# Graph attention on one core: edge chunks of 512 become 1024, node ranges 32 become 42, and the last stage is spread over the engines in another way

## The reference

```python
Q_h = (x @ Wq + bq).reshape(N, H, D)          # N 12500, H 8, D 12
K_h = (x @ Wk + bk).reshape(N, H, D)
V_h = (x @ Wv + bv).reshape(N, H, D)
E = (edge_attr @ We + be).reshape(-1, H, D)
src = K_h[src_idx]
dest = Q_h[dst_idx]
score = src * dest / sqrt(D) * E
score = exp(clip(score.sum(-1, keepdims=True), -5.0, 5.0))
msg = V_h[src_idx] * score
wV = segment_sum(msg, dst_idx, num_segments=N)
Z = segment_sum(score, dst_idx, num_segments=N)
h_out = wV / (Z + 1e-06)
out = layernorm(x + h_out)
```

## Time and profile before

| what | us |
|---|---|
| median of 3 runs (lowest, highest) | 5353.9 (5344.9, 5357.64) |
| the profiled execution | 5341.94 |
| its span in the trace | 5340.3 |
| busy: PE, DVE, ACT, POOL | 3563.3, 2090.0, 1722.8, 3143.5 |
| first gather of the loop's steady part to the last one | 143.44 to 5217.30 |
| last stage | 5245.00 to 5340.30 |

### The profile page before, as it was taken

How to read it: one execution, slowest core, us unless ns; L and a number is a source line. 1 busy time by engine, 2 the same in 40 slices (tenths; PEclk the granted TensorE clock), 3 DMA queues, 4 the chain that set the end, 5 groups by cost and what they waited for, 6 DMA issues and landing times.

```text
span 5340.3 us, 72730 instructions
## 1 busy us (share of the span) xinstructions
PE 3563.3 (67%) x19972; PEld 3422.0 (64%) x19973; DVE 2090.0 (39%) x5996; ACT 1722.8 (32%) x3602; POOL 3143.5 (59%) x3249
## 2 busy tenths in 40 slices
PE   7666666666666666666666666666666666666664
PEld 6666666666666666666666666666666666666663
DVE  4333334333333333333333433333334333433346
ACT  4332333323332332333233332333333232323337
POOL 4556656665666656656665666566566665666560
PEclk7555555555555555555555555555555555555555
DMA  7444444444444444444444444444444444444442
GB/s 227 107 109 110 119 109 109 111 118 109 109 111 117 110 108 111 116 111 109 111 116 112 109 112 113 113 109 111 110 118 109 110 115 113 109 110 116 112 109 84
DMA packets 497768, 607.49 MB, mean 114 GB/s; under 512 B 256053, under 2 KB 420224, under 8 KB 497630
## 3 DMA queue, kind: packets, MB, share of 16 engines
q0 software_dynamic: 155200, 318.39, 22.5%
q1 hardware_dynamic: 233215, 281.36, 18.0%
q10 hardware_dynamic: 109330, 7.48, 1.5%
HBM read 584.51 MB, written 22.46 MB: 114 GB/s over the span
## 4 chain that ended last, share of the span: by engine, by line
PE 51%; issue 27%; another core or an unknown queue 13%; DVE 4%; ACT 2%; DVEq 1%; DMA 0%; ACTq 0%; POOL 0%; SPq 0%; POOLq 0%
PE bank L633 18%; PE bank L647 17%; PE bank L631 11%; PE bank L640 5%; DVE kqe L915 2%; DVE raw_score L926 1%; DVEq L303 1%; ACT spare L814 0%; DVE oh L910 0%; ACT spare L802 0%; ACT accP L792 0%; PE bank L597 0%; ACT eaT L760 0%; DVE kqe L907 0%
## 5 line engine op out<-in xcount | busy, mean ns | idle before, releaser
L530 POOL DMA_INDIRECT kv<-kv_table,src_idx x3224 | 3118.9, 967 | 2059.6 <-DVE msg L919 1020.4
L633 PE MATMUL bank<-w_e,eaT 97*128 97x96 f32 x6448 | 1886.1, 391 | 282.1 <-issue 282.1
L631 PE MATMUL bank<-ident,ea 128*96 128x128 f32 x3224 | 1354.9, 421 | 920.4 <-issue 610.5
L633 PEld LDWEIGHTS bank<-w_e,eaT 97*128 97x128 f32 x6448 | 1778.6, 333 | 290.4 <-issue 288.8
L907 DVE TENSOR_TENSOR kqe<-kv,bank 128x384 f32<-128x384 f32 x806 | 446.4, 554 | 3157.5 <-remote 2428.7
L631 PEld LDWEIGHTS bank<-ident,ea 128*96 128x96 f32 x3224 | 806.2, 250 | 928.7 <-issue 594.5
L647 PE MATMUL bank<-oh,msg 128*104 128x32 f32 x6448 | 1276.8, 355 | 172.3 <-issue 170.0
L647 PEld LDWEIGHTS bank<-oh,msg 128*104 128x104 f32 x6448 | 1225.4, 290 | 168.7 <-issue 166.0
L757 ACT ACTIVATE msg<-score 128x32 f32<-128x32 f32 x806 | 184.8, 229 | 3504.8 <-remote 2565.3
L640 PEld LDWEIGHTS bank<-q_win,ohT 96*128 96x128 bf16 x3224 | 398.3, 154 | 414.5 <-issue 408.2
L640 PE MATMUL bank<-q_win,ohT 96*128 96x96 bf16 x3224 | 448.5, 279 | 299.6 <-issue 295.5
(11 more groups left out here) (81 smaller groups left out, 525.8 us busy)
## 6 DMA issues: line engine op xcount, KB each, us to landing
ea<-in_edge_attr_dram SPq DMA_DIRECT2D x201, 768.0 KB
dst_b<-dst_by_chunk SPq DMA_DIRECT2D x201, 384.0 KB
kv<-kv_table,src_idx POOLq DMA_INDIRECT x3224
q_win<-q_table SPq DMA_DIRECT2D x806, 19.9 KB
kv_table<-kv_out SPq DMA_DIRECT2D x25, 336.0 KB
q_table<-q_out SPq DMA_DIRECT2D x25, 252.0 KB
spare<-in_x_dram SPq DMA_DIRECT2D x25, 168.0 KB
out_dram<-spare SPq DMA_DIRECT2D x25, 168.0 KB
```

What stands on the lines that cost most here:

```text
L530: pool.indirect_dma_start(kv[:, slot, g, :], None, kv_dram[:, :], bass.IndirectOffsetOnAxis(ap=src_idx[:, u, g:g + 1], axis=0)).then_inc(k ...
L631: last = nc.tensor.transpose(eaT_ps[u % 2][0:D, g * P:(g + 1) * P], ea[:, u, g, :], ident[:, :])
L633: nc.tensor.matmul(e_ps[v % 2][:, g * D:(g + 1) * D], eaT[:, v % 2, g * P:(g + 1) * P], w_e[:, :], start=True, stop=True)
```

## The change

Chunks have 1024 edges (`G` = 8, `C` = 403) and node ranges 42 nodes. Rings have 4 slots (`RING`), halves 2 (`HALF`), so they hold as many edges as before. The pipeline is arranged anew: a PE step `s` turns chunk s and raises `pe_turned`, sums chunk s - 2, picks the Q rows of chunk s, projects chunk s, and raises `pe_projected`. `eaT`, `eaT_ps`, `e_ps` and `q_ps` have one buffer each, of twice the size. ACT's step waits on `pe_turned`, DVE's and SP's on `pe_projected`. DVE's step computes scores and messages of the same chunk. In the last stage PE turns `accT` directly, POOL adds the residual, and mean and variance come from DVE's `bn_stats` and `bn_aggr`. In the diff, the parts are those of SP, POOL, PE, DVE in the loop, and DVE in the last stage, in this order.

```diff
-G = 4
+G = 8
+GB = 4
 CHUNK = P * G
-WIN = 32
+WIN = 42
-PROJ_LAG = 2
-SUM_LAG = 5
+SUM_LAG = 2
-RING = 8
+RING = 4
 HALF = RING // 2
+ROUND = 8
...
             def half_round(s, h, bases):
-                sp.wait_ge(pe_step, s - HALF + PROJ_LAG)
+                sp.wait_ge(pe_projected, s - HALF)
                 sp.sem_inc(loads_allowed, 1)
...
+            def add_residual(b, u):
+                pool.wait_ge(y_attended, b + 1)
+                wait_batch(pool, x_res_in, b, u)
+                nc.gpsimd.tensor_tensor(y[0:NP, u, :, :], y[0:NP, u, :, :], x_res[0:NP, u, :, :], ALU.add).then_inc(res_added, 1)
...
             def step(s, u, _):
-                c, v = s - PROJ_LAG, (u - PROJ_LAG) % RING
-                n, w = s - SUM_LAG, (u - SUM_LAG) % RING
+                n, w = s - SUM_LAG, (u - SUM_LAG) % 2
...
+                    for g in range(G):
+                        last = nc.tensor.transpose(eaT_ps[0:D, g * P:(g + 1) * P], ea[:, u, g, :], ident[:, :])
+                    last.then_inc(pe_turned, 1)
                 if summing:
                     pe.wait_ge(msg_ready, n + 1)
                     at_least(pe, acc_added, n - 1)
...
+                if whole:
+                    pe.wait_ge(ohT_built, s + 1)
+                    at_least(pe, kqe_done, s)
+                    landed(pe, q_win_in, s, u, 16)
...
+                        nc.tensor.matmul(edge_rows(q_ps, g), sel[:, g, :], q_win[0:SEL, u, :],
+                                         start=(g % GB == 0), stop=(g % GB == GB - 1), skip_group_check=True)
+                    pe.wait_ge(eaT_copied, s + 1)
+                    for g in range(G):
+                        last = nc.tensor.matmul(edge_rows(e_ps, g), eaT[:, g * P:(g + 1) * P], w_e[:, :],
+                                                start=True, stop=True)
-                last.then_inc(pe_step, 1)
+                last.then_inc(pe_projected, 1)
...
             def step(s, u, base):
-                dve.wait_ge(pe_step, a + PROJ_LAG + 1)
+                dve.wait_ge(pe_projected, s + 1)
...
+                    dve.wait_ge(heads_summed, s + 1)
+                    nc.vector.tensor_scalar(score[:, h, :], raw_score[:, :], -5.0, 5.0, ALU.max, ALU.min).then_inc(score_ready, 1)
+                    dve.wait_ge(exp_done, s + 1)
+                    nc.vector.tensor_tensor(msg[:, h, :, 0:D].rearrange("p g (h d) -> p g h d", d=HD),
...
                 if second:
-                    dve.wait_ge(squared, b)
-                    nc.vector.tensor_reduce(sq_sum[0:NP, v % 2, :], ysq[0:NP, v % 2, :, :], AX_X, ALU.add).then_inc(sq_summed, 1)
+                    dve.wait_ge(res_added, b)
+                    for j in range(BATCH):
+                        last = nc.vector.bn_stats(y_stats[0:NP, v % 2, j, :], y[0:NP, v, j, :])
+                    last.then_inc(stats_made, 1)
```

More of the change, by code:

```diff
@@ L31 @@
 NP16 = 112
+NQ16 = 96
 BATCH = 4
@@ L39, in at_least, with run_steps @@
         engine.wait_ge(sem, value)
-def run_steps(engine, step, chunks, lag, round_values=None, from_round=0, unroll=RING, ahead=0):
+def run_steps(engine, step, chunks, lag, round_values=None, from_round=0, unroll=ROUND, ahead=0):
     rounds = (chunks - 1 - ahead) // unroll
@@ L223, in gnn_kernel @@
         kv_in = [sem(f"kv_in{i}") for i in range(RING)]
-        pe_step = sem("pe_step")
+        pe_turned = sem("pe_turned")
+        pe_projected = sem("pe_projected")
         eaT_copied = sem("eaT_copied")
@@ L335, in within @@
         def within(node):
-            return nc.s_assert_within(node, 0, N - 1, skip_runtime_bounds_check_because=
-                                      "a chunk's windows end with the one that holds its greatest destination")
+            return nc.s_assert_within(node, 0, N_PAD - WIN, skip_runtime_bounds_check_because=
+                                      "a chunk's windows end with the one that holds its greatest destination or the next")
         def load_sources(engine, s, u):
@@ L626, in step @@
-                if projecting:
-                    pe.wait_ge(eaT_copied, c + 1)
-                    at_least(pe, kqe_done, c - 1)
-                for g in range(G):
-                    if turning:
-                        last = nc.tensor.transpose(eaT_ps[u % 2][0:D, g * P:(g + 1) * P], ea[:, u, g, :], ident[:, :])
-                    if projecting:
-                        nc.tensor.matmul(e_ps[v % 2][:, g * D:(g + 1) * D], eaT[:, v % 2, g * P:(g + 1) * P],
-                                         w_e[:, :], start=True, stop=True)
@@ L660, in add_queries @@
                     for g in range(G):
-                        last = nc.tensor.matmul(q_ps[0][:, g * D:(g + 1) * D], sel[:, g, :], q_win[0:SEL, 0, :],
-                                                start=first and g == 0, stop=(g == G - 1), skip_group_check=True)
+                        last = nc.tensor.matmul(edge_rows(q_ps, g), sel[:, g, :], q_win[0:SEL, 0, :],
+                                                start=first and g % GB == 0, stop=(g % GB == GB - 1), skip_group_check=True)
                     last.then_inc(f_q_added, 1)
@@ L754, in step @@
+            def step(s, u, _):
+                c, v = s - 1, (u - 1) % 2
+                coming = not isinstance(s, int) or s + 1 < C
+                if not isinstance(s, int) or s < C:
+                    act.wait_ge(pe_turned, s + 1)
+                    nc.scalar.copy(eaT[0:D, :], eaT_ps[0:D, :]).then_inc(eaT_copied, 1)
+                if coming:
+                    measure(s + 1, (u + 1) % RING)
                 if not isinstance(s, int) or 0 <= c < C:
                     act.wait_ge(score_ready, c + 1)
-                    nc.scalar.activation(msg[:, v % 2, :, D:DZ],
-                                         score[:, v % 2, :].rearrange("p (g h) -> p g h", g=G), ACT.Exp).then_inc(exp_done, 1)
@@ L930, in step @@
+                if not isinstance(s, int) or 0 <= n < C:
                     if base is None:
```

362 lines of the change are left out of this document (171 added, 191 removed).

## The result

The changed kernel takes 5725.56 us (median of 4, 5720.45 to 5741.11) against 5353.2: ratio 1.0701, 95% interval 1.0677 to 1.0725. The prediction was 5765. The profiled execution's span is 5721.7 us against 5340.3, so 381.4 us more.

The account below looks back on a forecast made before the run. The prediction took the loop as bound by PE's signals held until POOL's run of gathers ends, then DVE's chain before POOL restarts. 5341.9 + 439 + 5 - 8 - 24 = 5754, 5765 for the median; range 4600 to 5900.

Parts of the forecast that it names:

- The chain: DVE's work from PE's signal to the messages, uncovered while POOL's queue is empty: 4.7 us a period, against 1.69 before.
- The restart: POOL's time from DVE's messages to its next gather: 0.81 us a period.
- The first signal after a release: PE's signal due 0.9 us into the next run of gathers was to come on time.
- The release: Time from a run's last gather until PE's held signal reaches DVE: 2.29 us, as before.
- The sum of a period: Steady loop: 19.79 + 2.29 + 4.7 + 0.81 = 27.6 us against 25.56, put at +2.2, times 199.5 periods: +439 us.
- lower bound of 4600: Lower end of the forecast range, taking in mid-run cases down to a release at 16.5 us.
- The second signal: PE's next signal, 20.8 us into a run ending at 19.79, was to come with the release at 22.1 us.
- the first rival: PE's second signal comes in mid-run: total between 4270 and 5330 us, 4840 at the middle; chance 0.24.
- DVE holding POOL: Rival: DVE's message product in each run slows gathers, +65 to +100 us, up to 5865; chance 0.09.
- First chunks: Loop's start: the first step takes a whole 1024-edge chain, about +5 us.
- Last chunks: After the last gather: two PE steps at 8.5 us and the chain, about 20 us against 27.7: -8 us.
- The last stage: 25 batches after the loop, DVE at 2.7 us a batch: -24 us, with bounds of 0 and -45.

Follow-up runs that it names:

- e5: Changed kernel with POOL's gathers of chunk s also waiting for pe_projected of chunk s-3, and DVE's oh and accT add behind the clip: 5109.4 us, 0.9547 of the kernel before.
- c0: The changed kernel with no edit, as a base: 5714.1 us, 1.0681 of the kernel before.
- e1: Changed kernel with one more wait on POOL, gathers of chunk s also waiting for pe_projected of chunk s-3: 5114.8 us, 0.9383 of the kernel before.
- e10: Changed kernel with POOL filling 2048 columns after every 8 gathers, run where the kernel before takes 5351 us: 5291.4 us, 0.9892 of the kernel before.
- e2: Changed kernel with DVE's oh and add into accT moved behind the clip: 5619.1 us, 1.0285 of the kernel before.
- e3: Changed kernel with gathers of 96 floats a row instead of 192, so half the bytes: 5916.2 us, 1.0843 of the kernel before.
- e4: Changed kernel with PE's and DVE's loops unrolled over 4 chunks in place of 8: 5914.1 us, 1.0839 of the kernel before.
- e7: Changed kernel with ACT's exponential of chunk s-1 ahead of its wait for pe_turned of chunk s: 5906.0 us, 1.1026 of the kernel before.
- e8: Changed kernel with POOL filling 2048 columns of an unused tile after every 8 gathers: 5300.8 us, 1.2398 of a kernel before that took 4274.2 us.
- e9: Changed kernel with POOL filling 256 columns of an unused tile after each gather: 5302.8 us, 1.2403 of a kernel before that took 4274.2 us.
- e6: Kernel before with POOL also waiting, every second chunk of 512 edges, for the step that projects chunk s-5: 5174.4 us, 0.9665 of the kernel before.

## Why the prediction was right, and where it was off

**What bounds the loop** was read rightly: DVE's chain in POOL's idle time behind a signal held to the run's end. The gap at 2410.20 shows its three parts, the pauses' sum grew by 477.2 us, and with the chain beside gathers the kernel takes 605 us less (e5 against c0; e1 reached 5115 without DVE's other order). That PE's signals are held while gathers are issued, late in a run, and come out in a pause is shown by the phases (180 of 182, then 9 of 199) and by e10. The length of the chain itself was never changed by an experiment, as e2 missed; its share rests on the 4.73 us of the gaps. By what means the signals are held stays open.

**The chain**: 4.7 predicted, 4.73 measured. **The restart**: 0.81 and 0.81. **The first signal after a release**, due 0.9 us into the run by the prediction, was due at 1.1 and came on time.

**The release** was the term of the period that moved: 2.29 taken over from before, 1.56 at 2410.20, median 2.9 over the loop.

**The sum of a period** has a slip. 19.79 + 2.29 + 4.7 + 0.81 is 27.59, which is 2.03 more than 25.56 and not 2.2: the run falls from 20.77 to 19.79, by 0.98, where only the inner gap of 0.8 was counted. By its own terms the loop's growth is 405 us and not 439, so 34 of the 66 us by which the steady loop was missed are this slip. Nor is the period of before that was read the only kind: 135 of the steady loop's 218 runs have 16 gathers and 76 have 12. Its 25.56 agrees with the mean of 25.43 all the same. The lower bound of 4600 for a release at 16.5 us comes out at 4645 when it is worked out again.

**The second signal**: predicted to come with the run's end. It does in 155 of the 188 runs, which have 16 gathers; 27 runs have 24, as one signal came in mid-run, the first rival in part, and in 21 of the 187 gaps DVE had started before the run's end. So the predicted pause was met by luck: its mean in the steady loop is 7.82 against 7.8, but as the mean of usual ones of 8.4, with a later release, and of short ones behind mid-run signals. There are also 186 of them and not 198, which saves some 90 us. The steady loop grew by 372.5 us, 1.87 a period. Where no signal comes in mid-run (e3, e4, e7), a period is 28.2 to 28.3 us, more than my 27.6, since the release takes 3.1, 3.1 and 2.9 us there (medians); over 199.5 periods that is some 130 us more than 27.59 gives.

**DVE holding POOL**: not seen in the mean, 958 ns a gather against 967. Of 3224 gathers 74 took over 1.1 us, and 242 before.

**First chunks**: +5 predicted, +12.8. The pause before the 33rd gather is 35.25 us against 28.97, so 6.3 for the whole chain; the first gather of the loop also starts 5.6 us later (76.80 against 71.16), a term that the prediction doesn't have. **Last chunks**: -8 predicted, +9.1, the wrong sign. PE in the changed kernel after the last gather:

```profile
5608.52 3.69 PE L669 MATMUL e_ps<-w_e,eaT 97*128 97x96 f32 x16
...
5625.54 3.70 PE L669 MATMUL e_ps<-w_e,eaT 97*128 97x96 f32 x16
5629.03 2.89 PE L657 MATMUL sum_ps<-oh,msg 128*104 128x42 f32 x16
5634.06 3.00 PE L657 MATMUL sum_ps<-oh,msg 128*104 128x42 f32 x16 [2.14 <-DVE msg L951]
5639.46 0.79 PE L721 MATMUL eaT_ps<-ident,accT 104*125 104x104 f32 x2 [2.40 <-issue]
```

Three projections are left and not two, and behind them each chunk's chain runs alone: DVE's messages, then the sums of the last chunk.

**The last stage**: -24 predicted, -13.0. bn_stats and bn_aggr cost what was bounded (18.2 and 9.2 us in 25 batches, 1.1 us a batch). The group that explains the rest, of the changed kernel's last stage:

```profile
L1023 DVE TENSOR_TENSOR spare<-eaT_ps,z_inv 125x384 f32<-125x384 f32 x25 | 13.9, 557 | 14.1 <-DMA out_dram<-spare 13.6
```

DVE waits 13.6 us for stores that must have left a buffer before it is written again. DVE itself is busy for 57.7 us, 2.3 a batch, the low end of the 2.3 to 3.0 that was bounded. So the stores come late next; the prediction named no transfer there.

The misses, -66 in the steady loop, +8 and +17 at its ends and +11 in the last stage, add up to -30, and 5754 less 30 is the 5724 of the profiled execution, as it must be. Misses of both signs thus hide one another. Of the 12 us that were added for the median of the runs, which make the forecast 5765, only 1.8 came.

## What to carry to other kernels

Where an engine's signals come out only while another one pauses, as most did here, the chain between the signal and the pausing engine's restart is paid in full at each pause, so a longer step lost here although it has fewer instructions. Look for the earliest sign of progress that the pausing engine may wait for, and let it pause for that: an added wait gained 10% here, since the mean pause became 3.6 us (e1) in place of 8.0 and the chain moved beside work. Look at several periods before one is taken as the pattern, and add the terms of a difference up from both sums. A change that makes steps longer must also be costed at the loop's two ends.

## What was not expected of the hardware

The same kernel before took 5351 us on one chip, and on another 5455 and, beside e8 and e9, 4274 us, each within 0.5% of its median, with no edit between them. In the two traces of that last group, both of kernels with pauses, pe_turned was never late between 400 and 5100 us. What decides whether signals are held while gathers are issued stays open; half the gathers' bytes and half the loop's body left it as it was, and it happens with either chunk size (e6).

PE's granted clock was 0.50 on average over the loop before and 0.57 over the changed one's. After 9.0 us idle PE did a step at the lower of its two levels (0.50 from 2414.10 to 2418.20), in which 16 L669 matmuls took 3.69 us; they took 1.99 in the next step, at the higher (1.00, 2.4 GHz, from 2420.19 to 2427.01). PE was not the bound, but the clock shifts when the second signal falls due: 63 times 6 to 8.5 us into a run, always with the short L669 rows, and 119 times 8.5 to 11 us into it, always without. Of the early ones 20 were taken in mid-run and of the late ones 29, so what hangs on it is small if anything.
